# Keys masked to one head of a pair, and the slot transfers between query and key tiles removed

## The chip, the cores and the metric

The kernel runs on one core of one Trainium2 chip. The metric is the device time of one execution in microseconds (us). The engines are PE (TensorE), DVE (VectorE), ACT (ScalarE), POOL (GpSimd) and SP (SyncE, which here only issues transfers); each runs its own list of instructions in order, and semaphores order them against each other.

## The reference

Two layers; each is a gated cross attention followed by a gated mixture of experts. What the change touches is the attention, with 8 batches of 256 tokens, 16 heads of 16:

```python
def _L0_xattn_ref(query, key, value, Wq, bq, Wk, bk, Wv, bv, Wo, bo):
    q = (query @ Wq.T + bq).reshape(b, tq, NUM_HEADS, HEAD_DIM).transpose(0, 2, 1, 3)
    k = (key @ Wk.T + bk).reshape(b, tk, NUM_HEADS, HEAD_DIM).transpose(0, 2, 1, 3)
    v = (value @ Wv.T + bv).reshape(b, tk, NUM_HEADS, HEAD_DIM).transpose(0, 2, 1, 3)
    scores = jnp.einsum('bhqd,bhkd->bhqk', q, k) / np.sqrt(HEAD_DIM)
    attn = jax.nn.softmax(scores, axis=-1)
    out = jnp.einsum('bhqk,bhkd->bhqd', attn, v)
    out = out.transpose(0, 2, 1, 3).reshape(b, tq, EMBED_DIM)
    return out @ Wo.T + bo
...
x = x + jnp.tanh(g_xattn[0]) * _L0_xattn_ref(_layernorm(x), ctx_1024, ctx_1024, ...)
x = x + jnp.tanh(g_ffn[0]) * _L0_ffn_ref(_layernorm(x), ...)      # 8 experts, top 2
x = x + jnp.tanh(g_xattn[1]) * _L1_xattn_ref(_layernorm(x), ctx_1024, mask, ...)
x = x + jnp.tanh(g_ffn[1]) * _L1_ffn_ref(_layernorm(x), ...)      # 7 experts with a capacity
```

## The kernel before

The program has a short phase of constants, and then for each layer an attention phase, a routing phase and an expert phase, one after the other. The change is in the constants and in `attention_phase`.

The attention phase works batch by batch (`b` = 0 to 7). For each batch:

- `x_transpose`, `queries`, `keys` and `values` on PE project into one PSUM bank, `ps_lin`. ACT's `project` copies queries and keys out of it with their bias into the compact tiles `q_c` and `k_c`: 128 rows, 16 rows for each head, 8 heads in each of two columns `c`.
- Scores are computed twice. The first pass (`head_scores` 0 to 7) finds the maximum of each query's row. It works on pairs of heads in 32 rows: POOL rounds the queries to `q_r` (`round_queries`), ACT writes the keys twice to `k_r`, times 1 in one head of a pair and 0 in the other (`separate_keys`, the factor is `odd_head`), and DVE reduces the products (`take_maxima`). `max_transpose` on PE and `maxima` on ACT turn the negated maxima into rows of `m_t`.
- The second pass (`scores` 0 to 3, four heads each) writes the transposed scores with the maximum already subtracted. For that each head has a slot of 32 rows in `q_s` and `k_s`, of which 17 are used: 16 rows of the head and one row that holds the negated maximum on the queries' side and 1 on the keys' side. SP fills the slots by transfers: `queries_to_slots` and `keys_to_slots` issue eight each per batch, `maxima_to_slots` issues four.
- ACT takes the exponential (`probabilities` 0 to 3). PE multiplies with the values (`weigh_values`), ACT copies the result (`heads`), PE turns it (`turn_heads`), DVE divides by the sums (`normalise`). `o_transpose`, ACT's `outputs` and DVE's `outputs_low` prepare it for `out_project`.

The order on every engine is written out by hand: a start (batches 0 and 1 one ahead), a loop over `b` = 1 to 4 in which batch `b` is in its second pass, `b + 1` in its first and `b + 2` and `b + 3` are projected, and an end for batches 5 to 7. Nothing but these lists and the waits sets the order. The calls that the prediction speaks of stand in the loop like this, on ACT and on PE:

```python
                probabilities(b, 0)            # ACT
                keys(b + 2)
                separate_keys(b + 2)
                probabilities(b, 1)
                outputs(b - 1)
                heads(b, 0)
                inputs(b + 3)
...
                weigh_values(b, 0)             # PE
                o_transpose(b - 1)
                weigh_values(b, 1)
                head_scores(b + 1, 6)
                x_transpose(b + 3)
                scores(b, 2)
                head_scores(b + 1, 7)
                out_project(b - 1)
```

## Time and profile before

| | us |
|---|---|
| median of 3 runs | 910.2 |
| lowest and highest of them | 906.54, 913.91 |
| the profiled execution, its own time | 913.08 |
| its span | 911.3 |
| PE busy, share of the span | 791.0, 87% |
| DVE busy | 634.0, 70% |
| ACT busy | 467.3, 51% |
| POOL busy | 396.3, 43% |

The profiled execution took 913.08 us, 1.8 us more than its span from first to last instruction, and lies in the upper part of the three runs. Busy shares are means over phases with different limits; the attention phases lie at about 4 to 234 us and 552 to 777 us. "Granted clock" is the share of TensorE's full clock that the chip let through: 1.00 is 2.4 GHz, and 1.2 GHz shows as 0.50.

### The profile page before, as it was taken

Reading aid. Unit: us, or ns where it says so; the run is one execution under the profiler, and the core shown is the slowest. Engines: PE = TensorE matmul, PEld = TensorE weight load, DVE = VectorE, ACT = ScalarE, POOL = GpSimd, SP = SyncE. Lnnn points to the kernel's source line nnn. Section 1 sums busy time; section 2 is a strip of 40 time slices with the busy share of each in tenths; the row PEclk is TensorE's granted clock in tenths of the full one; section 3 lists DMA queues with packets and bytes.
Section 4 is the critical chain, followed back from the end, with each engine's and each line's share of the span. In section 5 each row is a group of like instructions: output and inputs, shape, how many; then the busy total and the mean of one; then the engine's idle time right before and its main releaser. Section 6 shows DMA issues by size and latency. Waiting matters only on the chain. (4 is left out here: it accounts for less than half of the span.)

```text
span 911.3 us, 17723 instructions
## 1 busy us (share of the span) xinstructions
PE 791.0 (87%) x6936; PEld 662.9 (73%) x6936; DVE 634.0 (70%) x1207; ACT 467.3 (51%) x696; POOL 396.3 (43%) x374
## 2 busy tenths in 40 slices
PE   5889999998438999999999975999999998348995
PEld 5566677656338999999999974666676656338995
DVE  3667776642658999999999932677776743758882
ACT  3256666444036766666667632166666542335540
POOL 4534453110134677777777443544543110232652
PEclk9779999888859999999999997699999988658998
DMA  7112111021166777887777527112111020775742
GB/s 218 37 37 60 51 50 44 8 74 39 49 235 241 220 243 236 242 237 240 238 240 239 139 30 209 40 38 62 51 51 40 13 83 25 203 185 195 231 85 32
DMA packets 57139, 113.74 MB, mean 125 GB/s; under 512 B 14176, under 2 KB 43360, under 8 KB 49376
## 3 DMA queue, kind: packets, MB, share of 16 engines
q0 software_dynamic: 20256, 69.43, 27.1%
q1 hardware_dynamic: 36800, 43.18, 15.6%
q8 instruction: 55, 0.90, 0.4%
q14 instruction: 28, 0.23, 0.1%
HBM read 85.17 MB, written 18.75 MB: 114 GB/s over the span
## 5 line engine op out<-in xcount | busy, mean ns | idle before, releaser
L563 DVE TENSOR_REDUCE mx_a<-ps_max_a 128x2 f32<-128x512 f32 x256 | 164.4, 685 | 67.8 <-PE ps_max_a L826 65.3
L73 PE MATMUL ps_h_e<-xe_t_e,w_e 128*128 128x256 f32 x480 | 141.3, 294 | 9.7 <-DVE xe_t_e L1659 9.7
L435 ACT ACTIVATE prob_a<-ps_st_a 128x2048 f32<-128x2048 f32 x64 | 120.1, 1876 | 54.8 <-PE ps_st_a L846 45.4
L75 PE MATMUL ps_h_e<-xe_t_e,w_e 128*128 128x256 f32 x480 | 138.0, 287 | 0.0
L74 PE MATMUL ps_h_e<-xe_t_e,w_e 128*128 128x256 f32 x480 | 138.0, 287 | 0.0
L73 PE MATMUL ps_y_e<-w_e,h_e 128*128 128x256 f32 x480 | 132.8, 277 | 0.0
L75 PE MATMUL ps_y_e<-w_e,h_e 128*128 128x256 f32 x480 | 132.7, 276 | 0.0
L74 PE MATMUL ps_y_e<-w_e,h_e 128*128 128x256 f32 x480 | 132.7, 276 | 0.0
L73 PEld LDWEIGHTS ps_h_e<-xe_t_e,w_e 128*128 128x128 f32 x480 | 95.6, 199 | 10.9 <-DVE xe_t_e L1659 10.9
L1503 POOL DMA_INDIRECT xe_e<-normalised_weighted,token_of x60 | 78.5, 1309 | 46.8 <-POOLq L61 19.8
L312 POOL TENSOR_SCALAR r_var_eps_a<-r_mean_var_a 128x2 f32<-128x2 f32 x16 | 3.7, 229 | 216.3 <-DVE r_mean_var_a L590 216.3
L74 PEld LDWEIGHTS ps_h_e<-xe_t_e,w_e 128*128 128x128 f32 x480 | 94.3, 196 | 0.0
L75 PEld LDWEIGHTS ps_h_e<-xe_t_e,w_e 128*128 128x128 f32 x480 | 93.9, 196 | 0.0
L1525 POOL DMA_INDIRECT x<-y_e,token_of x46 | 78.5, 1706 | 34.2 <-ACT y_e L1579 18.6
L75 PEld LDWEIGHTS ps_y_e<-w_e,h_e 128*128 128x128 f32 x480 | 90.1, 188 | 0.0
L73 PEld LDWEIGHTS ps_y_e<-w_e,h_e 128*128 128x128 f32 x480 | 90.1, 188 | 0.0
L74 PEld LDWEIGHTS ps_y_e<-w_e,h_e 128*128 128x128 f32 x480 | 90.1, 188 | 0.0
L846 PE MATMUL ps_st_a<-q_s_a,k_s_a 17*128 17x256 f32 x1024 | 84.1, 424 | 4.9 <-DMA q_s_a<-m_t_a 4.3
L1634 DVE TENSOR_TENSOR h_e<-hid_e,h_e 128x512 fp32r<-128x512 f32 x120 | 84.2, 702 | 4.1
L826 PE MATMUL ps_max_a<-k_r_a,q_r_a 32*128 32x512 f32 x256 | 81.6, 561 | 4.1 <-DVE mx_a L563 1.9
L1570 ACT ACTIVATE hid_e<-ps_h_e,b_e 128x256 f32<-128x256 f32 x184 | 77.5, 482 | 6.8 <-PE ps_h_e L75 6.8
L1552 ACT ACTIVATE w_e<-w_raw_w 128x1024 fp32r<-128x1024 f32 x60 | 64.4, 1076 | 28.9 <-PEq L61 28.9
(210 smaller groups left out, 1746.8 us busy)
## 6 DMA issues: line engine op xcount, KB each, us to landing
w_raw_w<-L_w SPq DMA_DIRECT2D x14, 1024.0 KB
ctx_raw_a<-ctx_t SPq DMA_DIRECT2D x16, 256.0 KB, 5.3
k_s_a<-k_c_a SPq DMA_DIRECT2D x128, 32.0 KB, 2.0
q_s_a<-q_c_a SPq DMA_DIRECT2D x128, 32.0 KB, 2.0
normalised_weighted<-xr SPq DMA_DIRECT2D x16, 256.0 KB, 2.3
x_sb<-x SPq DMA_DIRECT2D x2, 1792.0 KB
x<-x_sb SPq DMA_DIRECT2D x8, 256.0 KB, 2.5
out<-x_sb SPq DMA_DIRECT2D x8, 256.0 KB, 2.5
```

Of the source, the lines that this page charges most:

```text
L73: pe.matmul(out, lhs[0], rhs[0], start=start, stop=False)
L74: pe.matmul(out, lhs[1], rhs[0], start=False, stop=False)
L75: return pe.matmul(out, lhs[0], rhs[1], start=False, stop=stop)
L435: act.activation(prob[n % 2][:, :, :, :], ps_st[:, :, :, :], ACT.Exp, scale=HD ** -0.5).then_inc(prob_ready, 1)
L563: dve.tensor_reduce(mx[:, q, h + 2 * j:h + 2 * j + 2], ps_max[j][:, :, :], AX.X, ALU.max).then_inc(max_done, 1)
L826: pe.matmul(ps_max[j][:, :, :], q_r[b % 2][r:r + 32, c, q * P:(q + 1) * P], k_r[b % 2][r:r + 32, c, :, :], start=True, stop=True).then_inc ...
L846: ins = pe.matmul(ps_st[:, g, kt, :], k_s[b % 3][rows, c, kt * P:(kt + 1) * P], q_s[b % 3][rows, c, :], start=True, stop=True)
L1503: pool.indirect_dma_start(out=xe[b % 2][:, q, :], out_offset=None, in_=dram["xw"], in_offset=bass.IndirectOffsetOnAxis(ap=shared["token_of ...
L1525: pool.indirect_dma_start(out=dram["out" if layer else "x1"], out_offset=bass.IndirectOffsetOnAxis(ap=shared["token_of"][:, t:t + 1], axis=0),
L1552: act.activation(w1[b % 2][0][:, k, :, :], w1_raw[b % 2][:, k * F:(k + 1) * F].rearrange("p (j f) -> p j f", j=FC), ACT.Copy).then_inc(w1_ ...
L1570: ins = act.activation(hid[jp % 2][:, j, :], ps_h[jp % RB][:, j, :], ACT.Gelu, bias=b1[b % 2][:, 2 * jp + j:2 * jp + j + 1])
L1634: dve.tensor_tensor(h[b % 2][1][:, js, :], hid[jp % 2][:, :, :], h[b % 2][0][:, js, :].bitcast(F32), ALU.subtract).then_inc(h_ready, 1)
```

## The change

The heads are laid out in another order (`by_slot`), so that a pair of heads in 32 rows of the compact tile is also the pair of the second pass. The second pass then multiplies all 32 rows. For the first head of a pair the keys are the compact keys with the other head's 16 rows at zero, except that the other head's first row is 1; the queries are the compact queries, in which that same row has been overwritten by the negated maximum. For the second head of a pair it is the other way round. So there are two tiles of queries and two of keys for each batch, `q_s[b % 3][0 and 1]` and `k_s[b % 3][0 and 1]`, each 128x512.

- ACT writes the projected queries straight to `q_s[b % 3][0]` (there is no `q_c` any more). POOL rounds them as before and then copies them to `q_s[b % 3][1]`, a second instruction in `round_queries`.
- ACT writes both tiles of keys in a new function `mask_keys`, two instructions on 128x512 with a scale and a bias per row. It stands right behind `separate_keys` in all eight places of a layer.
- SP issues no query or key transfers. The four of the maxima stay, now into the overwritten row.
- PE's `scores` reads 32 rows instead of 17 and waits for `k_masked` instead of the transfers. DVE's `take_maxima` writes to other columns of `mx`.
- POOL's setting of `k_s` to 1 (`key_ones`) is gone. The constants gain four small DVE instructions for `one_row`.

The diff, cut to its core:

```diff
-            def to_slots(slots, compact, done):
-                for u in range(OCT):
-                    for g in range(HG):
-                        r = 64 * u + HD * g
-                        sp.dma_start(slots[32 * g:32 * g + HD, 2 * u:2 * u + 2, :], compact[r:r + HD, :, :]).then_inc(done, 16)
...
             def maxima_to_slots(b):
                 sp.wait_ge(mt_ready, b + 1)
+                sp.wait_ge(q_round, 2 * b + 2)
                 for c in range(CH):
-                    sp.dma_start(q_s[b % 3][HD:P:32, c, :], m_t[c * HG:c * HG + HG, :]).then_inc(m_ld, 16)
+                    first = HD if c % 2 == 0 else 0
+                    sp.dma_start(q_s[b % 3][c % 2][first:P:32, c // 2, :], m_t[c * HG:c * HG + HG, :]).then_inc(m_ld, 16)
...
             def round_queries(b):
                 wait(pool, s_ps, H * (b - 1))
+                wait(pool, st_ps, CH * (b - 2))
                 pool.wait_ge(q_evac, 2 * b + 2)
-                pool.tensor_copy(q_r[b % 2][:, :, :], q_c[b % 2][:, :, :]).then_inc(q_round, 1)
+                pool.tensor_copy(q_r[b % 2][:, :, :], q_s[b % 3][0][:, :, :]).then_inc(q_round, 1)
+                pool.tensor_copy(q_s[b % 3][1][:, :, :], q_s[b % 3][0][:, :, :]).then_inc(q_round, 1)
...
-            def project(b, ps_sem, evac, ld, bias, compact):
+            def project(b, ps_sem, evac, bias, out):
                 act.wait_ge(ps_sem, b + 1)
-                wait(act, ld[(b - 2) % 3], SLOTTED * ((b - 2) // 3 + 1))
...
+            def mask_keys(b):
+                wait(act, st_ps, CH * (b - 2))
+                for j in range(2):
+                    act.activation(k_s[b % 3][j][:, :, :], k_c[b % 2][:, :, :], ACT.Identity, scale=shared["odd_head"][:, j:j + 1],
+                                   bias=shared["one_row"][:, j:j + 1]).then_inc(k_masked, 1)
...
                 keys(b + 2)
                 separate_keys(b + 2)
+                mask_keys(b + 2)
                 probabilities(b, 1)
...
                     for g in range(HG):
-                        rows = slice(32 * g, 32 * g + HD + 1)
+                        rows = slice(32 * g, 32 * g + 32)
...
             dve.tensor_copy(shared["odd_head"][:, 1:2], odd[:, :]).then_inc(odd_ready, 1)
-            dve.wait_ge(odd_ready, 3)
+            dve.tensor_scalar(in_pair[:, :], shared["row_no"][:, :], 2 * HD - 1, None, ALU.bitwise_and).then_inc(odd_ready, 1)
+            dve.wait_ge(odd_ready, 4)
+            dve.tensor_copy(in_pair_f[:, :], in_pair[:, :]).then_inc(odd_ready, 1)
+            dve.wait_ge(odd_ready, 5)
+            for j in range(2):
+                dve.tensor_scalar(shared["one_row"][:, j:j + 1], in_pair_f[:, :], float(HD if j == 0 else 0), None,
+                                  ALU.is_equal).then_inc(odd_ready, 1)
+            dve.wait_ge(odd_ready, 7)
```

How the lists move at the places that the prediction speaks of. First ACT in the loop, before: `k_c` is `keys`, `k_r` is `separate_keys`, `prob` is `probabilities`, `o_t_hi` is `outputs`, `head_t` is `heads`, `xn_t_hi` is `inputs`.

```order
L435 ACTIVATE prob_a<-ps_st_a 128x2048
L389 ACTIVATE k_c_a<-ps_lin_a,bk_a 128x256 x2
L396 ACTIVATE k_r_a<-k_c_a,odd_head 128x2x256 x2
L435 ACTIVATE prob_a<-ps_st_a 128x2048
L429 ACTIVATE o_t_hi_a<-ps_lin_a 128x512
L441 ACTIVATE head_t_a<-ps_head_a 128x512
L413 ACTIVATE xn_t_hi_a<-ps_lin_a 128x512
L435 ACTIVATE prob_a<-ps_st_a 128x2048
```

The same place of ACT in the change:

```order
L410 ACTIVATE prob_a<-ps_st_a 128x2048
L359 ACTIVATE k_c_a<-ps_lin_a,bk_a 128x256 x2
L365 ACTIVATE k_r_a<-k_c_a,odd_head 128x2x256 x2
L382 ACTIVATE k_s_a<-k_c_a,one_row,odd_head 128x512 x2
L410 ACTIVATE prob_a<-ps_st_a 128x2048
L404 ACTIVATE o_t_hi_a<-ps_lin_a 128x512
L416 ACTIVATE head_t_a<-ps_head_a 128x512
L388 ACTIVATE xn_t_hi_a<-ps_lin_a 128x512
L410 ACTIVATE prob_a<-ps_st_a 128x2048
```

Two instructions stand between the split keys and the second exponential of the batch, and everything behind them on ACT is queued after them.

Then POOL near the start of a layer, before: `q_r` is `round_queries(0)`, the MEMSETs of `v` are `value_ones`, `ctx_t` is `split_context`.

```order
L293 TENSOR_SCALAR var_eps_a<-mean_var_a 128x2
L295 TENSOR_TENSOR rstd_a<-var_eps_a,minus_half_a 128x2
L336 CAST q_r_a<-q_c_a 128x512
L346 MEMSET v_a 128x32x16 x3
L329 CAST ctx_t_hi_a<-ctx_raw_a 128x512
L331 TENSOR_TENSOR ctx_t_lo_a<-ctx_raw_a,ctx_t_hi_a 128x512
```

The same place of POOL in the change:

```order
L268 TENSOR_SCALAR var_eps_a<-mean_var_a 128x2
L270 TENSOR_TENSOR rstd_a<-var_eps_a,minus_half_a 128x2
L312 CAST q_r_a<-q_s_a 128x512
L313 COPY q_s_a<-q_s_a 128x512
L318 MEMSET v_a 128x32x16 x3
L304 CAST ctx_t_hi_a<-ctx_raw_a 128x512
L306 TENSOR_TENSOR ctx_t_lo_a<-ctx_raw_a,ctx_t_hi_a 128x512
```

The copy of the queries stands ahead of the three MEMSETs, with no wait between them.

## Rows read from the trace of the kernel before

**Rows 1.** Windows: engines' busy us, then granted clock, DMA share, GB/s.
```profile
40.00:190.00 150.00, 144.65 (x1363) 98.71 (x1366) 103.36 (x203) 86.55 (x100) 52.66 (x61) 0.92 0.17 45
590.00:740.00 150.00, 145.43 (x1430) 99.42 (x1429) 107.20 (x209) 90.79 (x105) 53.16 (x61) 0.96 0.18 48
```

**Rows 2.** The page's groups, its DMA issues, and the SP queue's own waits.
```profile
L846 PE MATMUL ps_st_a<-q_s_a,k_s_a 17*128 17x256 f32 x1024 | 84.1, 424 | 4.9 <-DMA q_s_a<-m_t_a 4.3
...
k_s_a<-k_c_a SPq DMA_DIRECT2D x128, 32.0 KB, 2.0
...
SPq L222 <- ACT m_t_a L423: 102.5, 16, 21.4
```

**Rows 3.** Timeline of ACT, loop, b = 2: start us, us, engine, line.
```profile
97.87 1.34 ACT L396 ACTIVATE k_r_a<-k_c_a,odd_head 128x512 fp32r<-128x512 f32 x2
99.11 1.86 ACT L435 ACTIVATE prob_a<-ps_st_a 128x2048 f32<-128x2048 f32 x1
101.91 0.60 ACT L429 ACTIVATE o_t_hi_a<-ps_lin_a 128x512 fp32r<-128x512 f32 x1 [0.95 <-PE ps_lin_a L729]
...
104.04 0.60 ACT L413 ACTIVATE xn_t_hi_a<-ps_lin_a 128x512 fp32r<-128x512 f32 x1 [0.50 <-PE ps_lin_a L729]
```

**Rows 4.** Timeline of PE, the same batch.
```profile
101.81 1.07 PE L859 MATMUL ps_head_a<-prob_a,v_a 128*32 128x256 f32 x16
102.81 0.50 PE L826 MATMUL ps_max_a<-k_r_a,q_r_a 32*128 32x512 f32 x2
...
105.51 0.36 PE L73 MATMUL ps_lin_a<-wo_hi_a,o_t_hi_a 128*128 128x256 f32 x1 [0.19 <-DVE xn_t_lo_a L616]
```

**Rows 5.** Timeline of DVE, the same batch.
```profile
103.34 1.29 DVE L563 TENSOR_REDUCE mx_a<-ps_max_a 128x2 f32<-128x512 f32 x2
104.67 0.69 DVE L616 TENSOR_TENSOR xn_t_lo_a<-ps_lin_a,xn_t_hi_a 128x512 fp32r<-128x512 f32 x1
```

**Rows 6.** ACT on 128x512 from SBUF: a group by form, and one timeline row.
```profile
L396 ACT ACTIVATE k_r_a<-k_c_a,odd_head 128x512 fp32r<-128x512 f32 x12 | 8.0, 716 | 0.1
...
8.26 0.63 ACT L447 ACTIVATE wq_hi_a<-wq_raw_a 128x512 fp32r<-128x512 f32 x1 [5.61 <-DMA bq_a<-L_bq]
```

**Rows 7.** Timeline of ACT: `inputs(2)`, layer 0 and layer 1.
```profile
42.41 0.60 ACT L413 ACTIVATE xn_t_hi_a<-ps_lin_a 128x512 fp32r<-128x512 f32 x1 [0.69 <-PE ps_lin_a L729]
...
592.91 0.60 ACT L413 ACTIVATE xn_t_hi_a<-ps_lin_a 128x512 fp32r<-128x512 f32 x1 [0.98 <-PE ps_lin_a L729]
```

**Rows 8.** Timeline of ACT and PE: `heads(0, 0)` and `turn_heads(0, 0)`, layer 0.
```profile
63.95 0.59 ACT L441 ACTIVATE head_t_a<-ps_head_a 128x512 f32<-128x512 f32 x1
...
65.55 0.60 PE L868 MATMUL ps_head_a<-ident,head_t_a 128*128 128x128 f32 x4
```

**Rows 9.** Timeline of ACT and PE: `maxima(6)` and `scores(6, 0)`, layer 0.
```profile
176.09 0.37 ACT L423 ACTIVATE m_t_a<-ps_max_a 16x256 f32<-16x256 f32 x1 [0.70 <-PE ps_max_a L833]
...
180.10 1.12 PE L846 MATMUL ps_st_a<-q_s_a,k_s_a 17*128 17x256 f32 x13 [0.64 <-DMA q_s_a<-m_t_a]
```

**Rows 10.** Timeline of DVE and SP: end of the constants, first load of layer 0.
```profile
3.07 0.14 DVE L1080 CAST odd_head<-odd 128x1 f32<-128x1 int32 x1
...
4.14 0.39 SPq L225 DMA_DIRECT2D x_sb<-x  x1
```

**Rows 11.** Timeline of POOL, DVE and PE near the start of layer 0.
```profile
20.92 0.61 POOL L336 CAST q_r_a<-q_c_a 128x512 fp32r<-128x512 f32 x1
21.48 1.45 POOL L346 MEMSET v_a<- 128x512 f32 x3
...
21.00 2.07 DVE L545 TENSOR_SCALAR xn_a<-x_sb,mean_var_a,rstd_a 128x256 f32<-128x256 f32 x1 [0.93 <-POOL rstd_a L295]
...
25.35 1.09 PE L729 MATMUL ps_lin_a<-ident,xn_a 128*128 128x128 f32 x4 [1.56 <-DVE v_a L554]
```

**Rows 12.** Windows as in rows 1: `scores(0, 0)` to `x_transpose(3)`, layers 0 and 1.
```profile
47.40:60.50 13.10, 13.10 (x96) 9.20 (x96) 5.93 (x12) 4.62 (x5) 7.01 (x8) 0.61 0.25 62
597.30:606.00 8.70, 8.65 (x97) 6.43 (x98) 6.45 (x13) 5.82 (x6) 6.81 (x8) 1.00 0.21 47
```

More of the change, by code:

```diff
@@ L116, in attention_phase @@
         xn, xn_t = [sb(f"xn{i}", [P, QT, D]) for i in range(2)], halves("xn_t", [P, KC, S])
-        q_c, k_c = ([sb(f"{n}{i}", [P, KC, S]) for i in range(2)] for n in ("q_c", "k_c"))
-        q_s, k_s = ([sb(f"{n}{i}", [P, CH, S]) for i in range(3)] for n in ("q_s", "k_s"))
+        k_c = [sb(f"k_c{i}", [P, KC, S]) for i in range(2)]
+        q_s, k_s = ([[sb(f"{n}{i}{j}", [P, KC, S]) for j in range(2)] for i in range(3)] for n in ("q_s", "k_s"))
         q_r = [sb(f"q_r{i}", [P, KC, S], F32R) for i in range(2)]
@@ L146, in attention_phase @@
         normalised_first, routed_last = sem("normalised_first"), sem("routed_last")
-        key_ones_set, value_ones_set = sem("key_ones_set"), sem("value_ones_set")
-        q_ld, k_ld = ([sem(f"{n}{i}") for i in range(3)] for n in ("q_ld", "k_ld"))
+        value_ones_set = sem("value_ones_set")
+        k_masked = sem("k_masked")
         ctx_hi, ctx_split, xt_hi, ot_hi = (sem(n) for n in ("ctx_hi", "ctx_split", "xt_hi", "ot_hi"))
@@ L334, in round_queries @@
                 wait(pool, s_ps, H * (b - 1))
+                wait(pool, st_ps, CH * (b - 2))
                 pool.wait_ge(q_evac, 2 * b + 2)
-                pool.tensor_copy(q_r[b % 2][:, :, :], q_c[b % 2][:, :, :]).then_inc(q_round, 1)
-            def key_ones():
-                for i in range(3):
-                    ins = pool.memset(k_s[i][:, :, :], 1.0)
-                ins.then_inc(key_ones_set, 1)
+                pool.tensor_copy(q_r[b % 2][:, :, :], q_s[b % 3][0][:, :, :]).then_inc(q_round, 1)
+                pool.tensor_copy(q_s[b % 3][1][:, :, :], q_s[b % 3][0][:, :, :]).then_inc(q_round, 1)
             def value_ones():
@@ L350, in _ @@
             pool.wait_ge(pool_const, 1)
-            key_ones()
             rows_scale(0)
@@ L384, in _ @@
         def _(act):
-            def project(b, ps_sem, evac, ld, bias, compact):
+            def project(b, ps_sem, evac, bias, out):
                 act.wait_ge(ps_sem, b + 1)
-                wait(act, ld[(b - 2) % 3], SLOTTED * ((b - 2) // 3 + 1))
                 for c in range(KC):
-                    act.activation(compact[b % 2][:, c, :], ps_lin[:, c * S:(c + 1) * S], ACT.Identity,
-                                   bias=bias[:, c:c + 1]).then_inc(evac, 1)
+                    act.activation(out[:, c, :], ps_lin[:, c * S:(c + 1) * S], ACT.Identity, bias=bias[:, c:c + 1]).then_inc(evac, 1)
             def separate_keys(b):
@@ L399, in queries @@
             def queries(b):
-                wait(act, q_round, b - 1)
+                wait(act, st_ps, CH * (b - 2))
                 if b == 0:
                     act.wait_ge(wq_ld, 32)
-                project(b, q_ps, q_evac, q_ld, bq, q_c)
+                project(b, q_ps, q_evac, bq, q_s[b % 3][0])
             def keys(b):
@@ L459, in _ @@
             separate_keys(0)
+            mask_keys(0)
             inputs(1)
@@ L465, in _ @@
             separate_keys(1)
+            mask_keys(1)
             inputs(2)
@@ L474, in _ @@
             separate_keys(2)
+            mask_keys(2)
             heads(0, 0)
@@ L501, in _ @@
             separate_keys(B - 1)
+            mask_keys(B - 1)
             probabilities(B - 3, 2)
@@ L838, in scores @@
                 if c == 0:
-                    for slots_ld in (q_ld, k_ld):
-                        pe.wait_ge(slots_ld[b % 3], SLOTTED * (b // 3 + 1))
+                    pe.wait_ge(k_masked, 2 * b + 2)
                     pe.wait_ge(m_ld, 16 * CH * (b + 1))
@@ L844, in scores @@
                     for g in range(HG):
-                        rows = slice(32 * g, 32 * g + HD + 1)
-                        ins = pe.matmul(ps_st[:, g, kt, :], k_s[b % 3][rows, c, kt * P:(kt + 1) * P], q_s[b % 3][rows, c, :],
+                        rows = slice(32 * g, 32 * g + 32)
+                        ins = pe.matmul(ps_st[:, g, kt, :], k_s[b % 3][c % 2][rows, c // 2, kt * P:(kt + 1) * P],
+                                        q_s[b % 3][c % 2][rows, c // 2, :],
                                         start=True, stop=True)
```

35 lines of the change are left out of this document (10 added, 25 removed).

## The prediction

> **What bounds the kernel now.** I read the windows over both attention phases first, because the change lies nearly all in them [rows 1]. PE is busy 144.65 and 145.43 of 150 us, DVE about 105, ACT about 88, POOL 53. So PE sets the pace there, and what matters is only what makes PE wait longer or less, or work faster or slower. Next I asked what the removed transfers cost PE. The page's group of the second pass's matmuls shows 4.9 us of idle time ahead of them in the whole program, 4.3 of it for the transfer of the maxima, which stays [rows 2]. No wait of PE for the query or key transfers shows. ACT had waits for them too, in `project`, and none shows either: its idle times end on PE. SP's own longest wait of the attention phases is for the negated maxima from ACT, 102.5 us in 16 times [rows 2]: the queue stood ready and empty when the maxima came, so its 16 other issues per batch delayed nothing. The removed work was hidden. Then I read the timeline of one loop batch on ACT, PE and DVE, of eight alike [rows 3 to 5], to see what stands behind the place where the new ACT work goes in.
>
> **Removed.** The 256 slot transfers (128 of keys, as many of queries; [rows 2]) and `key_ones`: 0 us, by the above. What hides them is PE's work itself. The maxima go out no earlier, since SP had been waiting for them. I keep a gain from less traffic for the rivals.
>
> **PE's matmuls.** The count stays, and 32 rows take the place of 17 in the same four row blocks. The 16 recorded matmuls of a group of `scores` (8 in the code) run together. No row of before has this product with 32 rows; the nearest is the first pass, which uses 32 rows already, with 512 columns. I see nothing that makes 15 more rows of the same block longer, and take 0.
>
> **The price of `mask_keys`.** The nearest row is `separate_keys`, 128x512 from SBUF with one per-row operand: 716 ns each, and the pair with the start of what follows advances by 99.11 - 97.87 = 1.24 us, or 0.62 each, since neighbours overlap by about 0.09 [rows 3, 6]. The same size without a per-row operand took 0.63 [rows 6], so an operand costs 0.09. The new instructions have two, scale and bias: 0.72 + 0.09 = 0.81, and 0.72 each after the overlap. I take 1.43 us for the two. Bounds: 1.24 if the second operand is free, 1.62 if nothing overlaps.
>
> **In the loop (b = 1 to 4).** They push `probabilities(b, 1)` from 99.11 to 100.54; it ends 1.86 later at 102.40 instead of 100.97 [rows 3]. PE's `weigh_values(b, 1)` reads it and started at 101.81 [rows 4]. A hand-over to PE costs 0.15 where rows show it (`xn_t_lo` ends 104.67 + 0.69 = 105.36, its reader starts at 105.51 [rows 4, 5]), and one to DVE 0.03 (104.64 to 104.67 [rows 3, 5]). With 0.10 PE starts at 102.50, **0.69 late**. So 0.74 of the 1.43 is slack and the rest is a new wait. `outputs(b - 1)` comes 0.46 late, less than PE. Then `head_scores(b + 1, 6)`, directly behind `weigh_values` at 102.81 [rows 4], and the reduction of it on DVE, which runs to 103.34 + 1.29 = 104.63 and holds back `inputs_low` at 104.67 [rows 5]: all move by nearly the full 0.69. `out_project` already waits 0.19 for `inputs_low` [rows 4]. I see no wait behind it that is not for work that moves too, so nothing gives the delay back. I take 0.67 a batch, 4 batches, 2 layers: **5.4 us**. By the bounds of the price, 0.50 to 0.88 a batch.
>
> **In the start.** Batch 0's masks fall into an idle stretch of ACT and cost nothing. Batch 1's stand ahead of `inputs(2)` and `maxima(0)`. ACT idled 0.69 ahead of `inputs(2)` in layer 0 and 0.98 in layer 1 [rows 7]; with the overlap of 0.09 the slack is 0.78 and 1.07, and the delay 1.43 - 0.78 = 0.65 and 0.36. It goes to the maxima, on which the next `head_scores` waits. Batch 2's stand ahead of `heads(0, 0)`, which had started at 63.95 without idle time: it now ends at 63.95 + 1.43 + 0.59 = 65.97, and `turn_heads(0, 0)` moves from 65.55 to 66.07, 0.52 late [rows 8]; twice, 1.04. Together **2.05 us**.
>
> **In the end.** Batch 7's masks stand ahead of `probabilities(5, 2)` and so of `maxima(6)`, ahead of which ACT idled 0.70 [rows 9]: about 0.05 of overlap on top of it, so 0.68 late. `scores(6, 0)` was already waiting 0.64 for those maxima [rows 9], so it takes on 0.68; PE itself comes late by at most 1.43, 0.79 beyond its old wait, so the two nearly agree. Twice: **1.36 us**.
>
> **POOL's copy.** One more 128x512 instruction per batch, at 0.61 like the rounding [rows 11]. In the loop POOL is busy 53 of 150 us [rows 1] and it costs nothing. At the start it does: DVE's first `xn` instruction of batch 1 took 2.07 us, from 21.00 to 23.07, and POOL ran the rounding and the three MEMSETs without a gap until 21.48 + 1.45 = 22.93 [rows 11]. DVE stood still until POOL came to a pause. PE waits 1.56 us for what DVE does next, `v_a` [rows 11]. The copy stands in that unbroken piece, so DVE, PE and all behind come 0.61 late in each layer: **1.2 us**. The Trainium skill, "SBUF — State Buffer", section "SBUF: two separate sides", gives the rule: VectorE in some of its modes and GpSimd lock one shared pair of ports for a whole instruction, and the other blocks; the row agrees, and by a plain sharing of bandwidth the term would be near 0 and the sum 1.2 us less. The same section says that a DMA cannot slow a compute instruction, nor the reverse; by that, the rival below in which less traffic speeds PE gives nothing.
>
> **Constants.** DVE's cast ends at 3.21, and the phase ends on it: the first load of layer 0 is issued at 4.14 [rows 10]. Four more small instructions of 0.14, in three steps with a wait between them: 3 x 0.17 = **0.5 us**. Bounds 0.3 to 0.6.
>
> **Sum.** 5.4 + 2.05 + 1.36 + 1.2 + 0.5 = **10.5 us**. Against the profiled execution of 913.1 us that is 923.6. It is not the middle of the three runs; the same 10.5 on their median of 910.2 gives **920.7**, which I forecast. With 1.24 for the masks, and neither the copy nor more than 0.3 for the constants, the sum is 0.50 x 8 + 0.63 + 0.66 + 0.98 + 0.3 = 6.6; with 1.62 and all else at its upper end 13.4. So 916.8 to 923.6, before the clock and the spread of runs (906.5 to 913.9).
>
> **The clock.** Windows over the same work in both layers show what its state costs: from `scores(0, 0)` to `x_transpose(3)` layer 0 took 13.1 us at a granted clock of 0.61, layer 1 8.7 us at 1.00 [rows 12], so 4.4 us for about 10.2 us at the lower level (0.39 of the full clock missing, twice that share of the stretch). Ahead of it PE had waited for the maxima in both. Shifted by 1 to 3 us, such a stretch may come or go in either layer: 4.4 us either way, which is as wide as the spread of runs.
>
> **Rivals.** (1) *The exponential was not what PE waits on next, or gets its time back.* If the 0.74 of slack in the loop were really 1.4, as it would be if `weigh_values` started its weight loads late for another reason, the loop and end terms vanish and 10.5 - 6.8 = 3.7 remains: 913.9. For it: half of ACT's time is idle. Against it: the start times of reader and writer leave only 0.84 between them, and the eight loop batches repeat these times.
> (2) *Not slower: the wider matmuls keep the clock up.* In the attention windows the clock is 0.92 and 0.96 [rows 1], that is 24 and 12 us at the lower level. At 4.4 us for each 10.2 these cost 15.5 us. If these stretches went with 32 rows in place of 17, the result would be 910.2 + 10.5 - 15.5 = 905.2. It breaks even when two thirds of them, 24 us, go. Against it: in layer 0's stretch of [rows 12] PE had just waited for the maxima, which the change leaves as it is, and no row shows that the width of a matmul matters to the clock.
> (3) *A stretch at the lower clock is added*: a new wait of PE ahead of a sparse piece, 920.7 + 4.4 = 925.1.
> (4) *The transfers did cost something*: PE's second-pass groups took 424 ns a matmul with them in flight [rows 2]. Even 3% on the 290 us of PE work in the two windows [rows 1], 8.7 us, would only bring 912.0. No row shows PE slower while they run.
> (5) *The slots remain in some form*: SP's list in the change has no such transfer. I give it no chance.
>
> **How the numbers follow.** The sum as worked out 0.62; rival 1 0.12; rival 2 0.06; rival 3 0.12; rival 4 0.06; 0.02 left. About 1% is what a measurement of this kernel can tell from no change: 901.1 and 919.3. The forecast is 1.4 us above that bound. Of the sum's 0.62 I put 0.38 above 919.3 and 0.24 below, of rival 3 all above, of rivals 1, 2 and 4 nearly all within: slower 0.51, same 0.43, and faster 0.06 for a clock that does better than I can argue. The range goes from 912.5, which takes in most of rival 1, to 927, which takes in rival 3 and the upper bound of the terms.
>
> **What the profile after would show.** The two `k_s` instructions at about 0.81 us each (0.72 would say that the second operand is free); `probabilities(b, 1)` to `weigh_values(b, 1)` with PE idle about 0.7 on ACT's `prob`; a loop batch longer by 0.67 us; the first `xn` of batch 1 at 2.7 us; no change in the group of `scores` beside the clock; SP idle; waits of PE for the maxima as before. The forecast is wrong if the period of the loop stays, if the `scores` matmuls change their length at equal clock, or if the granted clock over the attention windows leaves 0.90 to 0.97.

## The result and the profile after

The changed kernel took **894.32 us** (median of 4 runs, 891.76 to 897.58), the kernel before 908.37 (4 runs, 903.73 to 913.91). The ratio is 0.9856, with a 95% interval of 0.982 to 0.9892: faster by 1.4%. The forecast was 920.7, slower. The profiled execution took 897.58 us, the slowest of the four, with a span of 895.8 and a mean granted clock of 0.927. Ratios here and below come from the single runs, without the few that lie over 1.5% above the fastest of their kernel, so they are not exactly the quotients of the medians.

First the windows over both attention phases in the kernel after, as [rows 1] (start and end of the window, its length, then busy us of PE, weight loads, DVE, ACT and POOL with their instruction counts, granted clock, DMA share, GB/s). The two further rows are what I call the ends of the two attention phases from here on: from the first to the last `router_inputs` after the loop, that is the end of batch 4's work and batches 5 to 7.

```profile
40.00:190.00 150.00, 142.09 (x1406) 97.74 (x1409) 106.36 (x208) 96.79 (x117) 56.53 (x67) 0.97 0.08 25
590.00:740.00 150.00, 142.75 (x1489) 98.00 (x1491) 102.47 (x204) 99.43 (x115) 58.96 (x69) 1.00 0.08 27
155.94:224.66 68.72, 62.11 (x623) 42.84 (x624) 35.94 (x77) 34.31 (x35) 9.04 (x13) 0.95 0.10 33
694.50:759.93 65.43, 59.09 (x623) 40.70 (x624) 35.91 (x77) 34.29 (x35) 9.02 (x13) 1.00 0.10 34
```

The same ends in the kernel before, which [rows 1] do not cover:

```profile
156.99:232.71 75.72, 69.69 (x623) 46.19 (x624) 35.87 (x77) 33.23 (x32) 8.66 (x12) 0.84 0.12 36
702.35:775.11 72.76, 66.79 (x623) 45.05 (x624) 35.87 (x77) 33.02 (x32) 8.66 (x12) 0.88 0.12 38
```

Here is most of the gain. PE runs the same 623 recorded instructions in each row. They took 75.72 and 72.76 us at a clock of 0.84 and 0.88, and take 68.72 and 65.43 at 0.95 and 1.00: 14.3 us less. The two profiled executions differ by 15.5 us. Another 4.7 are the stretch of [rows 12] in layer 0, which is not there after (from `inputs(2)` to `inputs(3)`, 19.84 us before and 15.17 after), and the new waits below take some back. Two groups of `scores` show what a level does, the first of PE's timeline before, the second of the timeline after:

```profile
209.84 2.09 PE L846 MATMUL ps_st_a<-q_s_a,k_s_a 17*128 17x256 f32 x16
```
```profile
204.24 1.15 PE L826 MATMUL ps_st_a<-q_s_a,k_s_a 32*128 32x256 f32 x16
```

At the full clock such a group takes 1.15 us in both kernels, in two places of a loop batch up to 1.36, again in both; 2.09 is the lower level. So the wider matmuls are no shorter by themselves; the page's group of them goes from 424 ns each to 400 [rows 2] by the clock alone:

```profile
L826 PE MATMUL ps_st_a<-q_s_a,k_s_a 32*128 32x256 f32 x1024 | 78.3, 400 | 5.9 <-DMA q_s_a<-m_t_a 2.7
```

The costs that the forecast named are there. ACT's timeline after in loop batch b = 2, as [rows 3], then PE's and DVE's, as [rows 4, 5]:

```profile
95.31 1.34 ACT L365 ACTIVATE k_r_a<-k_c_a,odd_head 128x512 fp32r<-128x512 f32 x2
96.56 1.51 ACT L382 ACTIVATE k_s_a<-k_c_a,one_row,odd_head 128x512 f32<-128x512 f32 x2
97.97 1.86 ACT L410 ACTIVATE prob_a<-ps_st_a 128x2048 f32<-128x2048 f32 x1
99.73 0.58 ACT L404 ACTIVATE o_t_hi_a<-ps_lin_a 128x512 fp32r<-128x512 f32 x1
101.01 0.60 ACT L416 ACTIVATE head_t_a<-ps_head_a 128x512 f32<-128x512 f32 x1 [0.71 <-PE ps_head_a L840]
101.99 0.60 ACT L388 ACTIVATE xn_t_hi_a<-ps_lin_a 128x512 fp32r<-128x512 f32 x1 [0.38 <-PE ps_lin_a L710]
```
```profile
99.88 1.07 PE L840 MATMUL ps_head_a<-prob_a,v_a 128*32 128x256 f32 x16 [0.55 <-ACT prob_a L410]
100.88 0.49 PE L807 MATMUL ps_max_a<-k_r_a,q_r_a 32*128 32x512 f32 x2
...
103.46 0.35 PE L73 MATMUL ps_lin_a<-wo_hi_a,o_t_hi_a 128*128 128x256 f32 x1 [0.20 <-DVE xn_t_lo_a L597]
```
```profile
101.41 1.29 DVE L544 TENSOR_REDUCE mx_a<-ps_max_a 128x2 f32<-128x512 f32 x2 [0.38 <-PE ps_max_a L807]
102.62 0.69 DVE L597 TENSOR_TENSOR xn_t_lo_a<-ps_lin_a,xn_t_hi_a 128x512 fp32r<-128x512 f32 x1
```

The two masks advance ACT by 97.97 - 96.56 = 1.41 us, and PE waits 0.55 us for the exponential behind them, where it waited for nothing. The reduction, `xn_t_lo` and `out_project` come late behind it, in the order that the forecast gave. The period of a loop batch, between two `xn_t_hi` rows of ACT, grew from 21.76 to 22.26 us: 0.50. The list of waits has the eight loop batches in one row, and SP's wait for the maxima, which was 102.5 us in 16 times [rows 2], now holds what had been its transfers:

```profile
PE ps_head_a L840 <- ACT prob_a L410: 4.4, 8, 0.6
```
```profile
SPq L207 <- ACT m_t_a L398: 289.4, 16, 21.5
```

The constants, as [rows 10]: DVE ends at 3.71 in place of 3.21, and SP issues at 4.64 in place of 4.14. That is the 0.5 us forecast.

```profile
3.07 0.14 DVE L1063 CAST odd_head<-odd 128x1 f32<-128x1 int32 x1
3.13 0.14 DVE L1064 TENSOR_SCALAR in_pair<-row_no_i 128x1 int32<-128x1 int32 x1
3.31 0.15 DVE L1066 CAST in_pair_f<-in_pair 128x1 f32<-128x1 int32 x1
3.50 0.21 DVE L1069 TENSOR_SCALAR one_row<-in_pair_f 128x1 f32<-128x1 f32 x2
```
```profile
4.64 0.39 SPq L210 DMA_DIRECT2D x_sb<-x  x1
```

### The profile page after: what moved, and what is told of

Same layout as the page of the kernel before. It is cut to its first block and busy times, and to the rows that moved or that the text cites. A ratio compares the mean times of both kernels' runs of the same rounds, so it can differ in the third digit from the quotient of the medians.

```text
span 895.8 us, 17491 instructions
## 1 busy us (share of the span) xinstructions
PE 775.1 (87%) x6936; PEld 657.3 (73%) x6936; DVE 632.4 (71%) x1211; ACT 487.8 (54%) x728; POOL 402.1 (45%) x384
## 3 DMA queue, kind: packets, MB, share of 16 engines
q1 hardware_dynamic: 28608, 34.78, 11.7%
## 5 line engine op out<-in xcount | busy, mean ns | idle before, releaser
L73 PEld LDWEIGHTS ps_h_e<-xe_t_e,w_e 128*128 128x128 f32 x480 | 95.5, 199 | 10.1 <-DVE xe_t_e L1649 10.1
L826 PE MATMUL ps_st_a<-q_s_a,k_s_a 32*128 32x256 f32 x1024 | 78.3, 400 | 5.9 <-DMA q_s_a<-m_t_a 2.7
L807 PE MATMUL ps_max_a<-k_r_a,q_r_a 32*128 32x512 f32 x256 | 78.4, 531 | 4.0 <-DVE mx_a L544 1.9
```

Source lines behind the costliest of these rows:

```text
L73: pe.matmul(out, lhs[0], rhs[0], start=start, stop=False)
L807: pe.matmul(ps_max[j][:, :, :], q_r[b % 2][r:r + 32, c, q * P:(q + 1) * P], k_r[b % 2][r:r + 32, c, :, :], start=True, stop=True).then_inc ...
L826: ins = pe.matmul(ps_st[:, g, kt, :], k_s[b % 3][c % 2][rows, c // 2, kt * P:(kt + 1) * P], q_s[b % 3][c % 2][rows, c // 2, :], start=True ...
```

## The experiments

The theories: **A**, 32 rows in place of 17 keep TensorE's clock up; **B**, the removed transfers had slowed something; **C**, the masks' new waits cost what the forecast says, or less because something gives it back. All ratios are to the kernel before, run on the same chip in the same job (medians 907.24 to 908.77 us).

| run | us, median | ratio, 95% interval | median clock of its runs | both ends of attention, us |
|---|---|---|---|---|
| kernel before | 907.86 (23 runs) | | 0.908 | 148.5 |
| the change | 894.32 | 0.9856 (0.982 to 0.9892) | 0.930 | 134.2 |
| e1, before, 32 rows | 892.18 | 0.9801 (0.9758 to 0.9844) | 0.9245 | 136.3 |
| e2, change, 17 rows | 907.62 | 0.9986 (0.9952 to 1.002) | 0.915 | 143.1 |
| e3, change, with transfers | 895.25 | 0.9861 (0.9816 to 0.9907) | 0.931 | |
| e4, masks later | 890.78 | 0.9804 (0.9765 to 0.9843) | 0.9275 | |
| e5, before, 24 rows | 896.02 | 0.9862 (0.98 to 0.9924) | 0.920 | 137.5 |
| e6, change, 17 and 32 | 897.79 | 0.9876 (0.9822 to 0.9929) | 0.927 | 133.8 |
| e7, before, extra pair | 909.45 | 1.0012 (0.9977 to 1.0047) | 0.916 | 143.4 |
| e8, change, two pairs | 927.05 | 1.0197 (1.0136 to 1.0258) | 0.909 | |
| e9, before, 32 in loop | 908.71 | 1.0004 (0.9969 to 1.004) | 0.9065 | 151.0 |
| e10, before, 32 at ends | 892.43 | 0.9829 (0.9776 to 0.9882) | 0.924 | 133.5 |
| e11, masks on POOL | 890.44 | 0.9832 (0.9791 to 0.9874) | 0.9245 | 131.6 |
| e12, masks, copy later | 891.29 | 0.9835 (0.9791 to 0.9879) | 0.926 | |
| e13, before again | 905.95 (one run) | | 0.909 | 148.4 |
| e14, extra pair, ends | 904.24 | 0.9988 (0.9958 to 1.0018) | 0.914 | 141.9 |
| e15, extra pair, loop | 913.65 | 1.0076 (1.0045 to 1.0107) | 0.906 | 145.8 |

The last column is the sum of the two windows from `router_inputs(3)` to `router_inputs(7)` in each profile, as in the six window rows above.

### Width, or transfers: e1, e2, e3

e1 is the kernel before with one number changed in `scores`; since 15 more rows are now read, POOL first sets `q_s` to zero, and SP waits for that once (`k_s` is set to 1 already).

```diff
+            def query_zeros():
+                for i in range(3):
+                    ins = pool.memset(q_s[i][:, :, :], 0.0)
+                ins.then_inc(query_zeros_set, 1)
...
-                        rows = slice(32 * g, 32 * g + HD + 1)
+                        rows = slice(32 * g, 32 * g + 32)
```

> The kernel before, with one thing changed: the second pass multiplies all 32 rows of each slot instead of 17 (the 15 spare rows of the queries are set to zero once, on POOL while it idles). Transfers stay, no masks. Theory A (the wider matmuls keep the granted clock up, and that is the whole gain): the clock of the profile rises from 0.90 to about 0.93, and since the masks' waits of some 6 to 10 us are absent, the time falls by 15 to 25 us, to 885 to 893. Theory B (the gain came from the removed transfers): the time and the clock stay as before, 904 to 914. Theory C (the gain came from other phases of the work against the clock's windows, that is from chance shifts): no systematic change, 900 to 915.

It took 892.18 us: the whole gain, and by the medians a little more, with all transfers in place.

e2 is the change with that line undone. It leaves most of the scores of every pair's second head out; the instructions and their order stay.

```diff
-                        rows = slice(32 * g, 32 * g + 32)
+                        rows = slice(32 * g, 32 * g + HD + 1)
```

> The changed kernel, but the second pass multiplies 17 rows again. For the second head of every pair this leaves its scores out (only the first of its rows is in the product), for the first head nothing is left out. Instruction counts and shapes of everything else stay. Theory A (the wider matmuls keep the clock up): the clock falls back to about 0.90 and the time rises to 914 to 920, above the kernel before, because the masks' waits stay. Theory B (removed transfers) and theory C (chance shifts): 890 to 900 as the changed kernel.

It took 907.62 us: nothing of the gain is left. e3 is the change with SP issuing as many and as large transfers again, into tiles that nobody reads.

```diff
+            def to_scratch(n, b):
...
+                        sp.dma_start(scratch[n][32 * g:32 * g + HD, 2 * u:2 * u + 2, :], w_raw["wq"][r:r + HD, :, :]).then_inc(
+                            scratch_ld[n], 16)
```

> The changed kernel plus the 256 slot transfers of the kernel before, same sizes, same places in SP's list and same waits, but into a scratch tile that nothing reads. Theory A (wider matmuls and the clock): within 3 us of the changed kernel, 891 to 898. Theory B (transfers slow PE or hold up loads): 904 to 912.

It took 895.25 us, 0.9 over the change and well inside the intervals. In its loop (89 to 155 us) the DMA share is 0.17 against 0.07 and PE's busy time 63.77 against 63.76 us. B falls. The Trainium skill, "SBUF — State Buffer", section "SBUF: two separate sides", says that a DMA cannot slow a compute instruction; these two numbers agree.

### Where the width acts: e9, e10

```diff
-                        rows = slice(32 * g, 32 * g + HD + 1)
+                        rows = slice(32 * g, 32 * g + (32 if 1 <= b < B - 3 else HD + 1))
```

> The kernel before with 32 rows in the second pass of batches 1 to 4 (the loop, where its granted clock is 1.00 already) and 17 in batches 0, 5, 6 and 7. With 32 rows everywhere it took 892.2 us, with 17 everywhere 907 to 909. If the gain is made in the sparse batches at the start and end of each attention phase, where the stretches at the lower clock stand, nothing is gained here: 905 to 909 us. If a wide matmul is simply shorter wherever it stands, or if the loop's rows decide what clock comes behind it, half or more of the gain shows: under 901.

e10 has the two numbers exchanged.

> The opposite of the run beside it: 32 rows in batches 0, 5, 6 and 7 and 17 in the loop. If the gain is made in the sparse batches, all of it shows: 891 to 895 us. Otherwise it stays over 900.

They took 908.71 and 892.43 us: the gain comes from batches 0, 5, 6 and 7, and none that shows (0.4% either way) from the loop. Both have e1's zeroing of `q_s`, so that is not what gains. The windows of the ends, e9, then e10:

```profile
152.91:228.10 75.19, 69.21 (x623) 46.63 (x624) 35.95 (x77) 33.26 (x33) 8.66 (x12) 0.84 0.12 37
695.09:770.89 75.80, 69.83 (x623) 46.48 (x624) 35.85 (x77) 33.23 (x32) 8.66 (x12) 0.84 0.12 36
```
```profile
152.39:219.33 66.94, 60.65 (x623) 41.62 (x624) 35.84 (x77) 33.03 (x33) 8.66 (x12) 0.97 0.14 41
688.32:754.88 66.56, 60.60 (x623) 41.58 (x624) 35.85 (x77) 33.02 (x32) 8.66 (x12) 0.97 0.14 41
```

The same instructions in the same order; only the rows of the `scores` matmuls in these batches differ, and with them the clock, 0.84 or 0.97. That is 17.5 us in these two profiles. What batch 0 adds, which lies outside these windows, is not tested apart. In the loop the clock was at 1.00 in the kernel before already (0.97 to 1.00 in the profiles between 90 and 155 us), so there was nothing to win.

### How much width: e5, e6

e5 is e1 with 24 rows (the first line below). e6 is the change with 17 rows in `scores` 0 and 2, where they hold all that is not zero, and 32 in 1 and 3 (the second line).

```diff
+                        rows = slice(32 * g, 32 * g + HD + 8)
```
```diff
+                        rows = slice(32 * g, 32 * g + (32 if c % 2 else HD + 1))
```

> The kernel before with 24 rows in the second pass (17 in the kernel before, 32 in the first experiment, where the time fell by 2% to 892.2 us and the mean granted clock of a run rose from 0.908 to 0.924). If each row of a matmul adds to what keeps TensorE's clock up, the time lies between: 7 of the 15 rows, so about 900 us (897 to 904) and a clock of about 0.915. If there is a step between 17 and 24 rows (for instance because a matmul of more than some number of rows is counted as whole), it is 892 as with 32; if the step lies above 24, it is 908 as before.

> The changed kernel with 17 rows in scores 0 and 2 (their heads' rows and the row of the maximum come first, the others are zeros) and 32 rows in scores 1 and 3. With 17 rows in all four it took 907.6 us and with 32 in all 894.3. If what counts is the number of wide matmuls, it lies half way, at about 901 us (898 to 904). If one narrow group is enough to lose the clock, it is 907; if every second wide group is enough to keep it, 894.

They took 896.02 and 897.79 us. By the medians 7 of 15 rows bring 11.2 us where e1 brought 16.5 (each against its own job's kernel before), and half of the groups bring 9.8 us of 13.3 (907.62 - 897.79 of 907.62 - 894.32). That 24 rows gain nothing, or half of the groups nothing, is out. The rest stays open: e5's interval reaches from 0.8% to 2.0%, and takes in both a share in proportion (0.9%) and all of e1's gain, and e6's, from 0.7% to 1.8%, takes in half and the whole as well. In e6's profile the ends are as short as with 32 rows everywhere (133.8 us).

### The masks' waits: e7, e8

e7 is the kernel before with an extra pair of ACT instructions of the masks' kind and size behind `separate_keys` in all places, into tiles that nobody reads. e8 is the change with the pair of masks doubled in the same way.

```diff
+            def dummy_masks(b):
+                wait(act, scratched, 2 * (b - 1))
+                for j in range(2):
+                    act.activation(scratch[b % 2][j][:, :, :], k_c[b % 2][:, :, :], ACT.Identity, scale=shared["odd_head"][:, j:j + 1],
+                                   bias=shared["odd_head"][:, j:j + 1]).then_inc(scratched, 1)
```

> The kernel before with two more instructions of ACT (128x512 from SBUF with a scale and a bias per row, into tiles that nobody reads) right behind the split keys in all five places: the waits of the masks alone, at 17 rows, with transfers. By the terms of the forecast (loop, start and end) it is slower by 8.8 us; with 0.50 instead of 0.67 a loop batch, as the trace of the change shows, by 7.4. So about 916 us against 908.6. If the clock gives part of it back, because PE is less dense, or the waits of start and end are absorbed behind them, it is under 912.

> The changed kernel with the pair of masks written twice (the added pair into tiles that nobody reads). The slack ahead of the second exponential is used up by the first pair (PE waits 0.55 us for it in each loop batch), so a second pair of 1.41 us goes to PE whole: 8 loop batches of 1.41 are 11.3 us, with start and end (three more places in each layer) up to 8 more, so 906 to 914 us against 894.3. If the first pair's wait of 0.5 us was given back later or by the clock, half of it or less shows: under 903.

e7 took 909.45 us, slower by 1.1 us with an interval of 3.2 either way, so the forecast's 8.8 is out as a net cost. Its trace has the waits all the same: the loop batch is 22.26 us long, and the first row below is e7's wait of PE. The second is e8's.

```profile
PE ps_head_a L872 <- ACT prob_a L443: 4.4, 8, 0.6
```
```profile
PE ps_head_a L846 <- ACT prob_a L416: 15.6, 8, 2.0
```

e8 took 927.05 us, 32.7 over the change, where I had expected 12 to 20. The waits are as forecast: 15.6 - 4.4 = 11.2 us, 1.40 a batch, so the slack was indeed used up. With three other waits for ACT at start and end, 20.2 us are added. The rest stands beside the clock. Windows of the loop, e8 in layer 0 and in layer 1, then the change in layer 0:

```profile
89.00:155.00 66.00, 62.09 (x578) 43.50 (x581) 41.35 (x86) 41.79 (x53) 32.75 (x39) 0.90 0.05 18
640.00:706.00 66.00, 61.48 (x620) 44.01 (x620) 45.23 (x95) 43.75 (x54) 32.89 (x39) 0.97 0.06 18
```
```profile
89.00:155.00 66.00, 63.76 (x664) 45.63 (x664) 46.28 (x94) 45.07 (x54) 32.27 (x38) 1.00 0.07 24
```

With waits of 2.0 us in a batch the clock no longer stays at its full level in the loop, where a wait of 0.55 had left it at 1.00. In the same 66 us of layer 0 PE got through 578 recorded instructions in place of 664. In layer 1, with the same waits, the clock is at 0.97 and the count at 620, so the loss differs from phase to phase.

### What gives the time back: e13, e14, e15

e13 is the kernel before once more, for a second profile. e14 has the extra pair of e7 only in batches 0, 1, 2 and 7, and e15 only in the loop.

> The kernel before, unchanged, for a second profile of it. If the stretch at the lower clock in layer 0 behind scores(0, 0) (13.1 us against 8.7 in layer 1) belongs to the kernel and not to that one execution, it stands here too; otherwise the window over the same work has the length of layer 1's, and the forecast's start terms were read from a disturbed place.

> The kernel before with the extra pair of ACT instructions in batches 0, 1, 2 and 7 only (start and end). The forecast's terms for the places are 2.05 and 1.36, 3.4 us in all: 912 against 908.7. If the waits in these places change where the stretches at the lower clock fall, and that gives more than it costs, it is at 906 or below, and the mean granted clock of a run is near 0.917 instead of 0.908.

> The kernel before with the extra pair in the loop's batches only. The trace shows 0.50 us a loop batch, so 4.0 us and 912.7; the forecast's 0.67 would be 5.4. If the end of a phase gives it back (its waits for DVE and ACT are there anyway), it is 909 to 910.

The window over the work of layer 0's [rows 12] row, from `scores(0, 0)` to `x_transpose(3)`, in e13 and then in e15, whose lists up to there are those of the kernel before:

```profile
48.20:56.80 8.60, 8.60 (x97) 6.34 (x97) 6.07 (x13) 4.73 (x5) 7.25 (x8) 1.00 0.22 49
```
```profile
47.40:62.00 14.60, 14.60 (x96) 10.45 (x96) 5.75 (x12) 4.61 (x5) 6.98 (x8) 0.53 0.22 56
```

The stretch that the forecast priced at 4.4 us comes in some executions and not in others: 8.6 us in e13, 13.1 in the profile that the forecast read, 14.6 in e15. With 17 rows in batch 0 it is also 8.6 in e2, e9 and e14, and 10.1 in e7; with 24 rows (e5) it is 11.7. With 32 rows it is 8.6 in seven profiles of seven without a second pair of masks (the change, e1, e3, e4, e10, e11, e12) and 9.3 in e8. Whether the width makes it rarer these few profiles don't decide. The ends' windows of e13 repeat (148.4 us at 0.84 and 0.88), so the low clock there belongs to the kernel. The profile that the forecast read was 5.2 us above the median of the kernel before (913.08 against 907.86), and this stretch is most of it.

e14 is 1.1 us faster by the ratio, at most 1.6 slower: the forecast's 3.4 for start and end is out as a net cost. e15 is 6.9 us slower (4.1 to 9.7), so the loop's 4.0 by the trace is real and not given back by itself. Where e7 makes up for it shows in its ends:

```profile
158.23:231.43 73.20, 66.71 (x623) 45.08 (x624) 36.00 (x77) 34.29 (x34) 8.64 (x12) 0.88 0.12 38
701.50:771.66 70.16, 63.61 (x623) 43.04 (x624) 36.00 (x77) 34.30 (x35) 8.63 (x12) 0.93 0.13 39
```

They take 143.4 us in place of 148.4, at 0.88 and 0.93 in place of 0.84 and 0.88, though PE waits longer for ACT there. e14 has about the same (141.9), and e2 (143.1). Profiles with 17 rows in the ends and no extra pair there vary by themselves: 145.8 (e15), 148.4, 148.5 and 151.0 (e9). So one extra pair of instructions ahead of `maxima(6)` goes with ends that are shorter by 2 to 9 us, at a higher clock. That the work of PE is displaced by the pair is what the three profiles have in common; that this is the cause is argued and not shown, nor why the clock takes it well here and badly in e8.

### Versions without the waits: e4, e11, e12

e4 puts each batch's masks where ACT idles, for example in the loop one batch later, behind `queries(b + 2)` (the first cut below). e12 is e4 with POOL's second copy of batch 0 moved behind `split_context(2)`. e11 leaves ACT alone and writes the masks on POOL (the second cut):

```diff
                 queries(b + 2)
+                mask_keys(b + 1)
                 heads(b - 1, 1)
...
                 separate_keys(b + 2)
-                mask_keys(b + 2)
```
```diff
+            def mask_keys(b):
+                wait(pool, st_ps, CH * (b - 2))
+                pool.wait_ge(k_evac, 2 * b + 2)
+                for j in range(2):
+                    pool.tensor_scalar(k_s[b % 3][j][:, :, :], k_c[b % 2][:, :, :], shared["odd_head"][:, j:j + 1],
+                                       shared["one_row"][:, j:j + 1], ALU.mult, ALU.add).then_inc(k_masked, 1)
```

> The changed kernel with each pair of mask instructions moved on ACT to a place where ACT idles for longer than they take: in the loop behind the next batch's queries (idle 1.68 us there in the changed kernel's trace), in the start behind the first maxima, in the end behind the second exponential of batch 6. If the masks cost what the trace of the changed kernel shows (the waits of PE for the exponential, 4.4 and 2.1 us, and about 0.5 us for every loop batch) the time falls by 5 to 8 us, to 886 to 890. If the delay is caught up elsewhere or the clock takes it back, 892 to 896.

> The changed kernel with its key masks written by POOL instead of ACT, in POOL's idle stretches (behind the split context of each loop batch, for the batch before). ACT then has nothing between the split keys and the second exponential, so the loop batch is 21.76 us again as in the kernel before, and starts and ends have no masks ahead of maxima and heads: 4 us less in the loops, and some 4 less beside them, so 887 us (884 to 891; the kernel with the masks later on ACT took 890.8). Against it: the masks are some 2.4 us each on POOL by the rows of its own per-row instructions, four times the length on ACT, and if POOL holds up DVE during them, as in the start of a layer, where a DVE instruction took 2.07 us instead of 0.6, the reductions of the first pass come late and it is 894 or more.

> The kernel with the masks later on ACT (890.8 us in the first job), and POOL's second copy of batch 0's queries moved from ahead of the ones of the values to behind the split of batch 2's context. The forecast charged that copy 0.6 us a layer; the trace of the change shows no longer DVE instruction for it, so by the trace nothing changes: 888 to 893 us. By the forecast's term it is 1.2 us less, 889.6, which the spread of runs hides; the start of DVE's instructions in the trace decides.

They took 890.78, 890.44 and 891.29 us: all three beat the change by 3 to 4 us in the medians, about the 4.0 of the loop's waits, and the kernel before by 1.7 to 2%. Against the change itself the ratios' intervals still overlap. My price for POOL's masks in e11 was wrong: 1.52 us for the pair, not 4.8 (twice the 2.4 of the expectation).

```profile
94.44 1.52 POOL L320 TENSOR_SCALAR k_s_a<-k_c_a,odd_head,one_row 128x512 f32<-128x512 f32 x2
```

Moving the copy changed nothing in the time that the runs could tell, and something in the trace: see POOL's copy below.

## Why the prediction was wrong

**The step that failed** is "PE's matmuls": "I see nothing that makes 15 more rows of the same block longer, and take 0." The length is indeed unchanged (1.15 us a group at the full clock). But the same words were used for the clock: rival 2 was set against with "no row shows that the width of a matmul matters to the clock", and got 0.06. No row could show it, because all matmuls of that kind in the trace had 17 rows; that was a reason to bound the effect, not to dismiss it. e1, e2, e9 and e10 show it: 32 rows in place of 17 are worth 13 to 17 us by the medians, and in the profiles 9 to 17 us of it stand in the ends of the attention phases (143.1 to 134.2 us from e2 to the change, 148.5 to 136.3 with e1, 151.0 to 133.5 from e9 to e10). Rival 2 had the size nearly right (15.5 us if the low stretches went), and that by luck: it took it from the windows of [rows 1], with the stretch of [rows 12] among them, which e13 shows to be absent in other executions. The ends, at 0.84 and 0.88, stood only half in those windows and I read no row for them.

**The clock as a condition.** "The forecast is wrong if [...] the granted clock over the attention windows leaves 0.90 to 0.97": it did, with 1.00 in layer 1. The two other signs did not come: the period of the loop grew, and the matmuls kept their length at equal clock.

**The price of `mask_keys`** was right: 1.51 us for the pair and 1.41 to what follows, against 1.43.

**The loop** was mis-sized: 0.50 us a batch against 0.67, 4.0 against 5.4. Counted from the start of the split keys, `weigh_values(b, 1)` came 3.94 us later before (101.81 - 97.87, [rows 3, 4]) and 4.57 after (99.88 - 95.31): 0.63 late against 0.69, the hand-over being 0.05 and not 0.10. The other 0.13 is taken up elsewhere in the batch; I haven't traced where. From `inputs(3)` to `inputs(4)`, which holds batch 2's masks as well as the first loop batch, a layer grew by 0.82 us (20.03 to 20.85), so 0.32 are left for batch 2's in place of 0.52. The mechanism, the place and the order of those that come late were right, and rival 1 (the exponential is not what PE waits on next) is out: e8 shows that each further microsecond there is paid, and more.

**Start and end**, 2.05 + 1.36: the new waits are there, and smaller. PE's waits for ACT outside the loop's `weigh_values` grew by 1.5, 0.4 and 0.6 us (`scores` for the exponential from 0.6 to 2.1, `head_scores` for the maxima from 0.7 to 1.1, `turn_heads` from nothing to 0.6), 2.5 in all against 3.4. As time they show less still: e10 and the change differ in the ends by 134.2 - 133.5 = 0.7 us, against 1.36. With 17 rows the ends with the extra pair are the shorter ones (e7, e14, e2), so there the clock gives more than the wait costs. e14 bounds the net of both terms at 1.6 us.

**POOL's copy**, 1.2 us, was wrong in its mechanism. Start of layer 0 in the change, POOL and DVE, as [rows 11]:

```profile
21.80 0.61 POOL L312 CAST q_r_a<-q_s_a 128x512 fp32r<-128x512 f32 x1
22.36 0.67 POOL L313 COPY q_s_a<-q_s_a 128x512 f32<-128x512 f32 x1
22.98 1.58 POOL L318 MEMSET v_a<- 128x512 f32 x3
```
```profile
21.88 1.30 DVE L525 TENSOR_SCALAR xn_a<-x_sb,mean_var_a,rstd_a 128x256 f32<-128x256 f32 x2 [0.93 <-POOL rstd_a L270]
...
24.60 0.69 DVE L534 TENSOR_TENSOR v_a<-ps_lin_a,bv_a 128x512 f32<-128x512 f32 x1 [0.48 <-POOL v_a L318]
```

And in e13, without the copy:

```profile
22.12 0.61 POOL L336 CAST q_r_a<-q_c_a 128x512 fp32r<-128x512 f32 x1
22.68 1.45 POOL L346 MEMSET v_a<- 128x512 f32 x3
```
```profile
22.20 2.68 DVE L545 TENSOR_SCALAR xn_a<-x_sb,mean_var_a,rstd_a 128x256 f32<-128x256 f32 x2 [0.92 <-POOL rstd_a L295]
```

DVE starts 0.08 us behind POOL's cast in both. With the copy next on POOL its two instructions take 1.30 us, with the MEMSETs next 2.68. It is so in both layers and in the profiles of e1, e2, e3, e11 and e12 as well; in e12, where the copy has moved away, it is 2.68 again. In batch 0 of the kernel before, where POOL was idle when each of the two began, the same pair took 0.73. Here is that row, and then the first of the two in the change alone:

```profile
9.09 0.73 DVE L545 TENSOR_SCALAR xn_a<-x_sb,mean_var_a,rstd_a 128x256 f32<-128x256 f32 x2 [1.17 <-POOL rstd_a L295]
```
```profile
21.88 0.68 DVE L525 TENSOR_SCALAR xn_a<-x_sb,mean_var_a,rstd_a 128x256 f32<-128x256 f32 x1 [0.93 <-POOL rstd_a L270]
```

So the cast and the copy held DVE up too, but each for its own length only: the first DVE instruction ends at 22.56, 0.15 us behind the cast (22.41), the second at 23.18, 0.15 behind the copy (23.03). Before, the first ended at 23.07, 0.14 behind the last of the three MEMSETs (22.93) [rows 11]. DVE was let in between the cast and the copy, and not between the cast and the MEMSETs or between these; why, no run shows. That POOL holds DVE up for a whole instruction, the rule that the forecast took from the Trainium skill ("SBUF — State Buffer", "SBUF: two separate sides"), agrees with these ends. What failed is the step from one instruction to an unbroken piece: the copy did not lengthen the piece by 0.61 but opened it, and DVE was done 1.4 us sooner. Behind it, PE's wait for `v_a` fell from 2.7 us in the two layers together (2.3 in e13) to 1.6, and is 4.0 in e12 against 1.3 in e4; the medians of these two, 0.5 us apart, don't show it.

**Constants**: right, 0.5.

**Transfers**: right, nothing (e3). **Rival 3** (a stretch of low clock added by a new wait) did not come about at a wait of 0.55 us; e8 shows it at 2.0.

In sum, the rest of the change costs 2.1 us by medians (the change against e1) or -1.2 (e2 against its kernel before, -4.4 to 1.8), in place of 10.5, and a gain of 13 to 17 us stands against it. Of the 8 us between by medians, 1.4 are the loop's size, 1.2 POOL's copy, and the rest the start's and end's terms and the clock, which e14 and e7 show together and don't part.

## What to carry to other kernels

Before costing a change of a matmul's shape at nothing because its duration stays, read the granted clock of each stretch of the phase, ends too. Here the ends at 0.84 and 0.88 had something to win by more rows, and the loop at 1.00 had not. Take a low stretch for the kernel's own only if a second profile has it. And do one part of the change alone first: a single number in one line was the whole of this one.

## What the runs showed of the hardware

- **The rows of a matmul mattered to TensorE's clock.** With the same instruction list, 32 rows in place of 17 in four of eight batches moved the clock of the ends from 0.84 to 0.97 (e9, e10), and the time by 16 us. The added products are all zero, in e1 of zeros and ones, in the change of queries and zeros (136.3 and 134.2 us in the ends); rows whose products are not zero were not tried. The Trainium skill, "TensorE: Matmul & The Clock Gate", section "What's actually happening", says that the clock goes by how busy PE has been and does not speak of rows. Here PE was busy 69.21 of 75.19 us with 17 rows and had the lower clock, and 60.65 of 66.94 with 32 (e9, e10). A lower clock lengthens the busy time itself, so these shares don't say how busy PE would be at one clock; but the instructions are the same, and where that section of the Trainium skill would have the two kernels alike, the measurement decides.
- **Short waits of PE cost about themselves, longer ones more.** 0.55 us a loop batch cost 0.50, with the loop's clock still at 1.00. In e8 PE's list of waits for ACT is longer than the change's by 20.2 us (15.6, 4.9, 4.5 and 3.4 against 4.4, 2.1, 1.1 and 0.6), and the time by 32.7; the rest stands beside a clock of 0.90 and 0.97 in place of 1.00 in the loops.
- **POOL's cast, copy and MEMSETs on 128x512 all held up DVE's two `xn` instructions.** The pair took 0.73 us where POOL was idle when each began, 1.30 beside the cast and the copy, and 2.68 where the MEMSETs followed the cast, since DVE was let in only behind the last of the three.
- **POOL's multiply-add with two operands per row took 0.76 us on 128x512**, hardly more than its copy (0.61), though its subtract-multiply takes 1.22 on 128x256. Why is open.
- ACT's second per-row operand cost 0.085 us: 801 ns with two, 716 with one.
